# Reordering the first microseconds of a two-layer gated cross-attention kernel, with new stage times throughout

## The reference, cut to what matters

```python
x = x + tanh(g_xattn[0]) * L0_xattn(layernorm(x), ctx)  # 16 heads of 16; q and k normalised per head
x = x + tanh(g_ffn[0])   * tanh(layernorm(x) @ w @ a1 @ a2 + bias)
x = x + tanh(g_xattn[1]) * L1_xattn(layernorm(x), ctx)  # 8 heads of 64; keys: own tokens and context
x = x + tanh(g_ffn[1])   * MoE(layernorm(x))            # 8 experts of 1024, top 2 of 8
```

## Time and profile before

| | |
|---|---|
| median of 3 runs | 602.05 us (599.68 to 603.24) |
| profiled execution, its own time | 603.49 us |
| its span, first to last instruction | 601.6 us |
| PE busy | 573.0 us (95%) |
| DVE busy | 402.7 us (67%) |
| ACT busy | 313.5 us (52%) |
| POOL busy | 272.5 us (45%) |
| first `S0` starts | 23.65 us |

### The profile page before, as it was taken

The page is one execution under the profiler, slowest core; times in us unless marked ns, Lnnn a source line. Parts: engine busy times, 40 slices in busy tenths (PEclk is TensorE's granted clock), DMA queues, the critical chain, the costliest instruction groups (busy, mean ns, idle before and its releaser), DMA issues.

```text
span 601.6 us, 13755 instructions
## 1 busy us (share of the span) xinstructions
PE 573.0 (95%) x5612; PEld 488.8 (81%) x5612; DVE 402.7 (67%) x819; ACT 313.5 (52%) x601; POOL 272.5 (45%) x238
## 2 busy tenths in 40 slices
PE   7989999999989999999999999999899999999994
PEld 6767677777756887988888888867899999989994
DVE  7785577678686565667666676667586777746651
ACT  2434554555555556555565555544445567636641
POOL 4338468559641064546555564640300344421324
PEclk9989999999999999999999999998899999999998
DMA  7910480000000000000000000037172677636112
GB/s 233 360 45 3 173 322 2 2 3 1 3 2 1 2 1 2 9 1 24 17 9 17 9 25 1 23 130 307 32 232 85 233 244 254 211 71 225 30 20 25
DMA packets 23803, 50.93 MB, mean 85 GB/s; under 512 B 7040, under 2 KB 16560, under 8 KB 20400
## 3 DMA queue, kind: packets, MB, share of 16 engines
q1 hardware_dynamic: 18272, 45.20, 20.7%
q0 software_dynamic: 4224, 3.70, 3.4%
q10 hardware_dynamic: 1232, 1.01, 0.6%
HBM read 37.89 MB, written 13.31 MB: 85 GB/s over the span
## 4 chain that ended last, share of the span: by engine, by line
PE 83%; DVE 9%; POOL 3%; ACT 2%; issue 2%; DMA 1%; POOLq 0%; ACTq 0%; DVEq 0%
PE ps L59 14%; PE ps L60 13%; PE ps L61 13%; PE ps L736 5%; PE ps L705 5%; PE ps L718 4%; PE ps L593 4%; DVE KN L1103 4%; PE ps L574 3%; PE ps L665 3%; PE ps L655 2%; PE ps L609 2%; POOL sr L1796 2%; PE ps L553 2%; PE ps L485 1%
## 5 line engine op out<-in xcount | busy, mean ns | idle before, releaser
L1841 POOL TENSOR_SCALAR P<-P,rinv 112x487 f32<-112x487 f32 x56 | 84.5, 1521 | 62.7 <-DVE rinv L1136 62.5
L60 PE MATMUL ps<-XGf,WH 128*128 128x256 f32 x252 | 71.3, 283 | 0.0
L61 PE MATMUL ps<-XGf,WL 128*128 128x256 f32 x252 | 71.3, 283 | 0.0
L59 PE MATMUL ps<-XGf,WH 128*128 128x256 f32 x252 | 71.3, 283 | 0.0
L1796 POOL TENSOR_TENSOR sr<-sv,mhalf 125x32 f32<-125x32 f32 x13 | 70.7, 5436 | 1.1
L406 POOL DMA_INDIRECT out<-WS,rows_i x16 | 28.4, 1776 | 89.1 <-ACT WS L1696 85.7
L1103 DVE TENSOR_REDUCE KN<-ps 112x4 f32<-112x1500 f32 x32 | 55.0, 1717 | 19.2 <-PE ps L574 19.2
L1451 DVE TENSOR_TENSOR WL<-WR,WH 128x1024 fp32r<-128x1024 f32 x48 | 57.1, 1220 | 13.4 <-ACT WH L1750 9.8
L1612 ACT ACTIVATE P<-ps,nm 112x487 f32<-112x487 f32 x64 | 42.1, 663 | 45.4 <-DVE nm L1128 41.8
L1563 ACT ACTIVATE P<-ps 125x1344 f32<-125x1344 f32 x32 | 41.3, 1292 | 42.1 <-PE ps L593 42.1
L1128 DVE TENSOR_REDUCE nm<-ps 112x1 f32<-112x487 f32 x64 | 39.5, 658 | 17.3 <-PE ps L705 17.3
(11 more groups left out here) (268 smaller groups left out, 1556.8 us busy)
## 6 DMA issues: line engine op xcount, KB each, us to landing
WR<-in_gupT SPq DMA_DIRECT2D x16, 1024.0 KB, 6.6
WR<-in_dwnT SPq DMA_DIRECT2D x8, 1024.0 KB, 10.1
xs<-ZT SPq DMA_DIRECT2D x14, 516.0 KB, 5.7
CT<-in_ctxT SPq DMA_DIRECT2D x1, 2250.0 KB, 10.3
P<-xs SPq DMA_DIRECT2D x7, 256.0 KB, 10.7
P<-xs SPq DMA_DIRECT2D x9, 128.0 KB, 2.6
Wk<-in_L_xattn_Wk SPq DMA_DIRECT2D x2, 512.0 KB, 11.9
Wv<-in_L_xattn_Wv SPq DMA_DIRECT2D x2, 512.0 KB, 12.0
```

Source lines behind the costliest of these rows:

```text
L59: e.matmul(out, ah, bh, start=start, stop=False)
L60: e.matmul(out, ah, bl, start=False, stop=False)
L61: return e.matmul(out, al, bh, start=False, stop=stop)
L1841: e.tensor_scalar(P[:, k, 0:487], P[:, k, 0:487], rinv[:, k:k + 1], None, ALU.mult).then_inc(s("psc"), 1)
```

## The change

- Tables: every planned time is new (`QUAD`, `FIRST`, `PREP`, ..., `WEIGHTS`), with a table `FFW` for the FFN product and `VALUES_1` for batch 1. Sorted, most engine orders stay; the pieces that move are named in the prediction.
- Weights' halves: SP loads the key half of Wkv first, then batch 0 of x alone, then the value half. Batches 1 and 2 of x, and the FFN matrices, go ahead of the large context transfer.
- Memsets: DVE clears KN[0] and only partitions 96 to 127, columns 256 to 511 of banks 5 to 7. The other banks are no longer cleared. V0[1], KN[1] and ZT move into a POOL stage `fill`, which waits for `roots` >= 3.
- Query factor: `qg` (POOL) multiplies the raw query by G before `ksc`; `qaff` only adds Bt, for b = 0 on DVE, otherwise on POOL, and its memset of the 17th column stays only for b >= 2.
- Sums: `kss` waits for the square alone (semaphore `sq`), not for the copy behind it.
- Centring of Wq is split in two stages, and ACT loads its function table with an early Tanh on `mhalf`.
- 24 instead of 30 filler transposes ahead of `spk` (0, 2).

```diff
-FIRST = ((-30, "stats0", 0), (-29.76, "rs0", 0), (-28.65, "wq"), (-24.69, "norm", 0, 0), (-15.7, "gain"),
...
+FIRST = ((-29.6, "stats0", 0), (-41.13, "rs0", 0), (-28.4, "wq", 0), (-19.85, "norm", 0, 0), (-18.21, "wq", 1),
+         (-17.07, "gain"), (-15.23, "qg", 0), (-8.16, "fill"), (2.74, "qg", 1), (-27.12, "kp", 0, 1, 0),
+         (-22.42, "kp", 0, 1, 1), (-13.94, "kq", 0, 1), (-24.56, "xt", 0, 0), (-15.54, "xtc", 0, 0),
+         (-21.19, "kp", 0, 0, 0), (-16.15, "kss", 0, 1), (-20.93, "kp", 0, 0, 1), (-13.27, "kq", 0, 0),
+         (-13.44, "kss", 0, 0), (-17.43, "v", 0, 0, 0), (-14.15, "v", 0, 0, 1), (-12.62, "vc", 0, 0),
+         (-12.55, "v", 0, 1, 0), (-9.39, "vc", 0, 1), (-13.22, "ksc", 0, 1), (-10.08, "spk", 0, 0),
+         (-10.6, "spkc", 0, 0), (-1.08, "spk", 0, 1), (-5.89, "spkc", 0, 1), (-13.59, "stats0", 1),
+         (-11.83, "stats0", 2), (-13.26, "ksc", 0, 0), (-12.09, "qaff", 0), (-11.87, "spk", 0, 2),
+         (-9.16, "spkc", 0, 2), (-7.0, "spq", 0), (-6.11, "spqc", 0), (-7.72, "rs0", 1), (17.01, "rs0", 2),
+         (-16.68, "kp", 1, 1, 0), (-9.92, "kp", 1, 1, 1), (-8.16, "kq", 1, 1), (-1.06, "kss", 1, 1),
...
-PAIR = ((0.31, "S"), (3.05, "sc"), (9.54, "T"), (13.18, "V"))
+PAIR = ((-0.08, "S"), (3.03, "sc"), (8.97, "T"), (12.95, "V"))
...
-WARM = {("kp", 0, 1, 0): 36, ("spk", 0, 2): 30, ("xt", NB - 1, 3): 18, ("rt4", NB - 1): 26, ("xin", 0): 62,
+WARM = {("kp", 0, 1, 0): 36, ("spk", 0, 2): 24, ("xt", NB - 1, 3): 18, ("rt4", NB - 1): 26, ("xin", 0): 62,
...
-            e.memset(ps[:, 5:8, :], 0.0).then_inc(s("dve0"), 1)
-            e.memset(ZT, 0.0).then_inc(s("dve0"), 1)
-            e.memset(ps[:, 2:4, :], 0.0).then_inc(s("dve0"), 1)
-            w.wait_ge(s("dve0"), 4)
-            e.memset(ZT.rearrange("p (a b) -> p a b", b=ROW)[:, :, D + 1:ROW], float(NO_ROW)).then_inc(s("dve0"), 1)
-            centre_weights(e, w, Wkv, "in_Wkv", PS_SET)
+            e.memset(ps[96:128, 5:8, 256:512], 0.0).then_inc(s("dve0"), 1)
+            centre_weights(e, w, Wkv, "in_Wk", ONES_SET + 1, range(2))
...
                 elif stage == "kss":
                     b, p = i
-                    for sem_, v in emptied(("kp", b, p, 0)):
-                        w.wait_ge(sem_, v)
+                    w.wait_ge(s("sq"), o_("kq", b, p))
...
                 elif stage == "ksc":
                     b, p = i
                     w.wait_ge(*scaled(b, p))
-                    w.wait_ge(s("pool0"), KN1_SET)
+                    if b:
+                        w.wait_ge(s("pool0"), KN1_SET)
+                    if p == 0:
+                        w.wait_ge(s("qg"), b + 1)
+                    for sem_, v in emptied(("kp", b, p, 0)):
+                        w.wait_ge(sem_, v)
...
+        def query_shift(e, w, b):
+
+            qn = heads(KN[b % 2][0:NQ, 3, :])
+            w.wait_ge(s("ksc"), o_("ksc", b, 0))
+            w.wait_ge(s("dve0"), G_SET)
+            if b >= 2:
+                e.memset(qn[:, :, 16:17], 0.0).then_inc(s("qaff"), 1)
+            e.tensor_tensor(qn[:, :, 0:16], qn[:, :, 0:16], Bt.rearrange("p (h d) -> p h d", d=16),
+                            ALU.add).then_inc(s("qaff"), 1)
...
+            w.wait_ge(s("pool0"), MH_SET)
+            e.activation(tg[:, 0:1], mhalf[:, 0:1], ACT.Tanh).then_inc(s("act0"), 1)
...
+                elif stage == "qg":
                     b, = i
...
+                    q = kraw[0:NQ, 0, 256:512]
+                    e.tensor_tensor(q, q, G, ALU.mult).then_inc(s("qg"), 1)
+                elif stage == "fill":
+                    w.wait_ge(s("roots"), 3)
+                    e.memset(V0[1], 0.0).then_inc(s("pool0"), 1)
...
+                    e.memset(KN[1], 0.0).then_inc(s("pool0"), 1)
...
+                    e.memset(ZT, 0.0).then_inc(s("pool0"), 1)
...
-            e.dma_start(Wkv[:, :, :], pk("L0_xattn_Wkv")).then_inc(s("in_Wkv"), 16)
-            e.dma_start(X[:, 0:2, :], A["x"][0:2].rearrange("b p d -> p b d")).then_inc(s("in_x0"), 16)
-
-            for what in ("in_Wkv", "in_ct0", "in_Wq"):
+            e.dma_start(Wkv[:, :, 0:256], pk("L0_xattn_Wkv")[:, :, 0:256]).then_inc(s("in_Wk"), 16)
+            e.dma_start(X[:, 0, :], A["x"][0]).then_inc(s("in_x0"), 16)
+            e.dma_start(Wkv[:, :, 256:512], pk("L0_xattn_Wkv")[:, :, 256:512]).then_inc(s("in_Wv"), 16)
+
+            for what in ("in_Wk", "in_ct0", "in_Wq"):
                 w.wait_ge(s(what), 16)
             e.dma_start(CT[:, :, 375:750], pk("ctxT")[:, :, 375:750]).then_inc(s("in_ct1"), 16)
-            e.dma_start(X[:, 2:NB, :], A["x"][2:NB].rearrange("b p d -> p b d")).then_inc(s("in_x"), 16)
+            e.dma_start(X[:, 1:3, :], A["x"][1:3].rearrange("b p d -> p b d")).then_inc(s("in_x1"), 16)
+            for k, n in enumerate(("L0_ffn_weight", "L0_ffn_aux_weight1", "L0_ffn_aux_weight2")):
+                e.dma_start(FW[k][:, :, :], pk(n)).then_inc(s("in_FW"), 16)
             e.dma_start(CT[:, :, 750:3000], pk("ctxT")[:, :, 750:3000]).then_inc(s("in_ct2"), 16)
+            e.dma_start(X[:, 3:NB, :], A["x"][3:NB].rearrange("b p d -> p b d")).then_inc(s("in_x"), 16)
```

More of the change, by code:

```diff
@@ L107 @@
-PREP = ((-36.62, "cs"), (-35.37, "norm", 0), (-32.44, "kp", 1, 0), (-32.74, "xt", 0), (-34.3, "xtc", 0),
-        (-29.47, "kp", 1, 1), (-28.27, "kq", 1), (-26.72, "kss", 1), (-26.6, "kp", 0, 0), (-23.9, "kp", 0, 1),
-        (-22.35, "kq", 0), (-21.2, "kss", 0), (-21.16, "ksc", 1), (-17.74, "spk", 0), (-17.8, "spkc", 0),
-        (-15.6, "spk", 1), (-15.1, "spkc", 1), (-13.77, "ksc", 0), (-13.74, "qaff"), (-9.86, "spq"), (-7.99, "spqc"),
-        (-7.96, "spk", 2), (-7.41, "spkc", 2))
-VALUES = ((-14.52, "v", 1, 0), (-13.63, "vc", 1), (-0.32, "v", 0, 0), (2.34, "v", 0, 1), (6.38, "vc", 0))
@@ new lines @@
+FIRST = ((-29.6, "stats0", 0), (-41.13, "rs0", 0), (-28.4, "wq", 0), (-19.85, "norm", 0, 0), (-18.21, "wq", 1),
[5 rows of a table added]
+         (-10.6, "spkc", 0, 0), (-1.08, "spk", 0, 1), (-5.89, "spkc", 0, 1), (-13.59, "stats0", 1),
+         (-11.83, "stats0", 2), (-13.26, "ksc", 0, 0), (-12.09, "qaff", 0), (-11.87, "spk", 0, 2),
+         (-9.16, "spkc", 0, 2), (-7.0, "spq", 0), (-6.11, "spqc", 0), (-7.72, "rs0", 1), (17.01, "rs0", 2),
+         (-16.68, "kp", 1, 1, 0), (-9.92, "kp", 1, 1, 1), (-8.16, "kq", 1, 1), (-1.06, "kss", 1, 1),
+         (-2.28, "norm", 1, 0), (1.28, "xt", 1, 0), (-5.02, "xtc", 1, 0), (2.33, "kp", 1, 0, 0),
+         (3.22, "kp", 1, 0, 1), (5.58, "kq", 1, 0), (6.47, "kss", 1, 0), (12.59, "ksc", 1, 1), (15.52, "spk", 1, 0),
+         (18.38, "spkc", 1, 0), (14.23, "spk", 1, 1), (13.63, "spkc", 1, 1), (11.2, "ksc", 1, 0), (10.65, "qaff", 1),
+         (12.14, "spk", 1, 2), (12.23, "spkc", 1, 2), (17.61, "spq", 1), (17.68, "spqc", 1))
@@ new lines @@
+PREP = ((-35.59, "cs"), (-37.56, "norm", 0), (-31.82, "kp", 1, 0), (-31.19, "xt", 0), (-30.89, "xtc", 0),
+        (-29.09, "kp", 1, 1), (-28.38, "kq", 1), (-24.82, "kss", 1), (-25.78, "kp", 0, 0), (-24.1, "kp", 0, 1),
+        (-20.82, "kq", 0), (-20.06, "kss", 0), (-19.87, "qg"), (-19.21, "ksc", 1), (-18.24, "spk", 0),
+        (-17.09, "spkc", 0), (-14.81, "spk", 1), (-15.81, "spkc", 1), (-10.92, "ksc", 0), (-15.34, "qaff"),
+        (-9.21, "spq"), (-9.2, "spqc"), (-8.4, "spk", 2), (-8.07, "spkc", 2))
@@ L176, in attention_order @@
         at(d, stage, *i)
[L177 to L178 removed]
+    for b in range(3, NB):
+        at(14.0 + 0.1 * b, "stats0", b)
     for b in range(NB):
         t = 4 * TQ * b
[L181 removed]
+        for d, stage, *i in (PREP if b >= 2 else ()) + (VALUES if b >= 2 else VALUES_1 if b else ()) + TAIL0:
             at(t + d, stage, b, *i)
[L183 to L184 removed]
+    for d, stage in FFW:
+        at(d, stage)
     for q in range(NQUAD):
@@ L1096, in vector_attention @@
                                     sr[:, p, :].unsqueeze(2).to_broadcast([125, 32, 16]), ALU.mult).then_inc(s("ksc"), 1)
+                elif stage == "qaff" and i[0] == 0:
+                    query_shift(e, w, 0)
                 elif stage == "spkc" and i[1] != 2:
```

133 lines of the change are left out of this document (62 added, 71 removed), and 9 rows, old and new, of tables (FIRST, FIRST1).

## The result

The changed kernel takes 598.25 us (median of 15 runs, 597.64 to 599.78), the kernel before 601.83 us (15 runs, 599.21 to 603.62). The ratio is 0.9951, with a 95% interval of 0.9936 to 0.9965: 3.6 us faster, and 0.15 from the 598.4 predicted. The profiled execution took 598.98 us, with a span of 597.2, against 603.49 and 601.6.

The account below looks back on a forecast made before the run. TensorE, with 83% of the chain that ended last, sets the pace, so gains need less work or fewer holes there. 1.5 + 1.85 + 0.3 + 0 = 3.65 us off the median 602.05 gives 598.4 us, range 596.8 to 600.2.

Parts of the forecast that it names:

- Part 1: Opening up to the first `S0`: 1.5 us sooner, at 22.1 us; bounds 0.7 and 2.0.
- Part 2: First to seventh `S0`: fewer TensorE holes and less slow clock gain 1.85 us; bounds 0.5 and 3.0.
- The half chance that the slow clock comes again: Before the fourth `S0`: slow clock as likely to recur as not, so half its 1.45 us counted, 0.7.
- Part 3: Steady first layer: small holes of 0.2 us per batch may close, gain 0.3 us; bounds -1.0 and 1.0.
- Part 4: Second layer: no TensorE hole from 195 to 400 us, end changed; gain 0, bounds -1.5 and 1.5.
- rival C: Second layer: copy ahead of the reciprocal makes `T` wait, 0.3 us in each of 28 pairs; 606.8 us; 9%.
- the stretch at 406 us: Near the second layer's end: the slow clock there cost 2.3 us in four groups.
- rival B: Holes shrink enough for full clock at 37 and 406 us: 6.7 us gained, 595.4 us; 13%.
- A: Start: DVE stays the bound, opening's gain waited away before the third maximum, only 1.2 us remains; 600.9 us; 20%.
- D: Opening: POOL's `fill` and DVE exclude each other, costing 2.9 us in the path of the roots; 601.3 us; 6%.

Follow-up runs that it names:

- experiment 4: Kernel before with the changed start alone: new code and order for batches 0 and 1, old order in the steady first layer and whole second layer; 606.23 us (1.0067).
- Experiments 7: Kernel after with DVE's two wide PSUM clearings back ahead of the weights' centring; 599.33 us (0.9961).
- 11: Kernel after with the key and value weights in one 512 KB transfer, as before, instead of two halves; 599.17 us (0.9973).
- experiment 9: Kernel before with 11 more TensorE fillers in the wait ahead of the transposes at 37.17 us; 601.61 us (0.9994).
- experiment 3: Kernel after with the old times of the first layer's steady part, query factor kept as its own stage just ahead of the first scaling; 612.12 us (1.0166).
- experiment 12: Kernel after with TensorE's transposes of the normalised x back behind the second `T` in six of eight second-layer batches, DVE's order kept; 599.35 us (0.9966).
- Experiment 5: Kernel after with the old order in the second layer's middle: score pairs 5 to 24, preparations of batches 2 to 6 and their tails; 603.99 us (1.0033).
- 8: Kernel after with 11 more TensorE fillers in the wait ahead of the transposes at 32.87 us; 599.41 us (0.9952).
- 10: Kernel after with 11 more fillers in the hole at 32 us, and 25 instead of 18 behind the last output projection; 598.39 us (0.9954).

## Why the prediction was right, and where it was wrong

**Part 1, predicted 1.5 us, measured 1.9** (first `S0` at 21.74 for 23.65; the eight profiles with this opening lie between 21.63 and 22.15). The landing of the key half, 4.8 us, was inside the bounds of 3.4 to 5.9, and centring ended at 6.9. Two terms were mis-sized. I had the 36 fillers take the same 6.66 us, and they took 5.89, so the first `kp` came at 7.32, not 8.24. But this didn't move the first `S0`. In the ten profiles with the new start the fillers took 5.70 to 7.07 us, and in nine of them the first `S0` stands 16.9 us behind the start of DVE's centring, whatever the fillers took; in experiment 4, with 7.07, it stands 17.1 behind it. The term that counts is `xt`. I had it start at 9.7, from 8.27 as the latest time for Wq, and it started at 9.13: Wq was there when DVE came to it at 7.49, and the chain on DVE (centring, statistics, half of Wq, normalisation, with the root on POOL under it) set the time. The query product then ended at 12.14 (12.8 predicted), DVE's first `ksc` at 17.40 (17.7), the fillers at 18.22 (18.9): still covered. From there to `S0` it took 3.5 us, not 3.25. The kernel before has its first `S0` 16.6 us behind the start of centring. So the opening gains by centring 2.27 us sooner, and its new order behind that loses 0.36. Experiments 7 and 11 show that the gain reaches the end, and that giving up either the narrow clearing or the split transfer costs about 1 us.

**Part 2, predicted 1.85, measured 1.93 in the profiled pair, which is luck.** The third maximum started at 32.69 (33.4), the seventh `S0` at 57.36 (57 to 59). The half chance that the slow clock comes again was a fair price, and it did come, five us earlier. But a pair of single profiles can't tell this step from the clock: against experiment 9, which has its half clock in the same place as the kernel after, the gain from first to seventh `S0` is 36.40 - 35.62 = 0.78 us.

**Part 3, a gain of 0.3 predicted, a loss of 0.7 measured.** It lies within the bounds (-1.0), but has the other sign. From the seventh `S0` to the second layer the lead shrinks from 3.84 to 3.10. Of this 0.42 is lost at one spot, the 28th `S0`, where the shift ended late (0.5 us of waiting of L572 for POOL), and some 0.08 per batch before it. Neither was tried alone; experiment 3 only shows that the old times would be worse with the new stages.

**Part 4, predicted 0 with bounds of 1.5 either way: this step failed twice, and the two errors left +1.3 us, inside the bounds by luck.** The steady second layer lost 1.45 us. "TensorE has no hole from 195 to 400 us: nothing to gain" was true, but there was something to lose, and the window still shows 204.96 of 205 busy, since the record of a product is drawn up to the next instruction over a wait of 0.15 us. The mechanism is close to that of rival C, the one I gave 9%: the reciprocal moves behind the copy. It moved by more than I took, because the residual's statistics come ahead of it too, and POOL then takes a root (0.9 us) before it divides. Against `S` the division starts 2.4 us later, which is more than the 1.75 to spare. C had `T` wait for it ahead of line 718. In the changed kernel TensorE waits one stage earlier, at `xt`, for the normalised x, which stands behind the same late root on POOL and behind the maximum on DVE; `T` waits for the division only where experiment 12 takes `xt` out of its way. And it happens mostly in one pair of a batch, at 0.19 us (6.66 for 6.47 us from this `S` to the next; five such pairs make 1.0 of the 1.45 us), not in 28 pairs at 0.3. Experiment 5 puts the old order back and gets 1.2 us over 18 pairs. Which of the moved stages on DVE would do it alone was not tried.

The end then gave 2.75 us back, from the 28th `S` to the end of the span. The profile of experiment 4 did as well with the old order and no half clock there, so this is the absence of the half clock at 406 and 426 us, and at full clock the new order of the end is worth nothing measurable. What it may be worth is fewer or cheaper stretches: with the new end and no upset border (after, 7, 8, 10, 11, 12) six profiles have no stretch at 406 us and two have one at 421 to 423, with some 208.0 us from the 28th `S` to the end; with the old end, two of three have both stretches and need 210.1 and 211.1. So few profiles don't settle it. I had priced the stretch at 406 us (2.3) for a loss or a gain, and put the gain with rival B only. That term, taken as zero, is where most of the 2.2 us of clock came from.

**The rivals.** A (the opening's gain is waited away) is refuted by experiments 7 and 11, though DVE does set the time of the first `S0`. B names the right source, though not its place: half clock remained at 32 us. D expected `fill` to exclude DVE's roots; the Newton operations beside it took 0.22 to 0.23 us each, as they did before without it, so that part is wrong. Its other half, `qg` against the roots' first step, is right: L1240 took 0.59 us in place of 0.20 and ended 0.05 us behind `qg`. In experiment 3 `ksc` took 1.23 us in place of 0.68 and ended 0.55 us behind POOL's multiplication. For this pair the trace agrees with the rule of the Trainium skill ("SBUF — State Buffer", "SBUF: two separate sides") that a DVE operation with two SBUF inputs and a GpSimd operation that reads SBUF exclude each other for a whole instruction. In the prediction I had read one pair, the power on POOL beside a context split on DVE, as evidence against it; that pair shows only that this power doesn't hold the split. In the changed kernel the price is 0.4 us, under the fillers.

So the sum of 3.65 stands against 3.6 with errors that cancel, and that is luck: 2.2 us lost in Part 3 and in the steady second layer, where I had a gain of 0.3, and 2.2 us of clock that I had at 0.7. In the profiled pair the parts add up to 1.91 + 1.93 - 0.74 - 1.45 + 2.75 = 4.4 us, more than the medians, because the profiled execution before is one of the slowest group. How the 1.4 us between runs at nearly full clock divide among the parts can't be read, since no profile shows the kernel before at full clock.

## What to carry to other kernels

Where one engine is "100% busy", ask which producers still have slack ahead of each of its stages, and by how much the change moves them: 1.75 us of slack was the number to watch, and busy time never showed its loss. In an opening, ask which start all later ones keep their distance to: here it was DVE's first operation on the weights, and the fillers ahead of the first product took anything from 5.70 to 7.07 us without changing that distance by more than 0.3. Tables of order don't mix well: all six mixtures of the two sets of tables ran slower than either kernel. And before a difference of half a per cent is explained, sort the runs of both kernels by their granted clock: the same instructions, with the same start times to 0.03 us, ran at full or half clock from one run to the next.

## What was not expected

A TensorE clock that falls for about 3.4 us to 0.5 at different places in runs of one program (32 or 37 us in the same instructions) makes three groups of times, 599.4, 601.9 and 603.2 us, in the kernel before. Why the changed kernel runs at 0.995 or more in 7 of 15 runs and the old one in 16 of 85, and which part of the change does it, is open. The same unsteadiness is there from the first microsecond: the 36 fillers at the start took 5.70, 5.79, 5.89, 5.98, 6.34, 6.53, 6.57, 6.89 and 7.07 us in different profiles, at a recorded clock of 1.00. They start 0.21 us apart up to a point and 0.11 us behind it, and this point moves: it came behind some 17 of them in the kernel after, behind some 28 in experiment 4. The ratio is that of the clock's two levels, but the record shows none of it. And POOL's shift of batch 1 took 2.74 us at 32.85 us in place of 0.73, while DVE ran a maximum and a scaling beside it, and 2.73 to 2.75 in all ten profiles with the new start; in later batches, with the maximum alone beside it, it took 0.73. It ended 0.6 us behind the scaling, although it had started 1.5 us ahead of it. Why it gave way is open.
